# A cross-attention kernel: q of block 1 used as projected, K and V in three passes, and other places for V and for the last part of q

## The reference

```
q = x @ wq;  k = ctx @ wk;  v = ctx @ wv
scores = (q . k) / sqrt(32), masked keys set to -inf
p = softmax(scores);  a = p @ v
out = layernorm(a @ wo + x) * gamma + beta
```

## Time and profile before

| | before |
|---|---|
| median of 3 runs (lowest to highest) | 627.19 us (625.45 to 628.61) |
| profiled execution: time, span | 628.64 us, 626.8 us |
| mean granted clock of TensorE | 0.993 |
| busy in the span: TensorE, VectorE, ScalarE, GpSimd | 602.5, 514.2, 501.8, 491.5 us |
| TensorE busy by stretch: 0 to 80, 80 to 168, 168 to 180 us | 71.27, 87.90, 9.31 us |
| the same: 180 to 560, 560 to 627 us | 378.39, 55.63 us |
| DMA: moved, mean | 91.31 MB, 146 GB/s |

### The profile page before, as it was taken

One profiled execution on the slowest core, in us unless ns is written; L12 is line 12 of the kernel. 1 busy time (PEld: TensorE's weight loads), 2 busy tenths in 40 slices (PEclk: granted clock), 3 DMA queues, 4 the chain that ended last, 5 costly groups with the idle time before them and its releaser, 6 DMA issues.

```text
span 626.8 us, 12867 instructions
## 1 busy us (share of the span) xinstructions
PE 602.5 (96%) x3820; PEld 472.4 (75%) x3820; DVE 514.2 (82%) x1047; ACT 501.8 (80%) x1546; POOL 491.5 (78%) x639
## 2 busy tenths in 40 slices
PE   7998999999999999999999999999999999998995
PEld 5776587887768778787878878787877878786763
DVE  3577588988868988898889888888888888888888
ACT  4578798888868888888978988898888888787851
POOL 4477359797958979797997979798887979687784
PEclk9999999999989999999999999999999999999999
DMA  8627365464554645554464645455454545643103
GB/s 290 193 51 204 111 165 152 147 166 131 155 169 119 171 120 167 147 168 141 125 183 136 171 136 167 135 150 162 138 162 111 167 143 145 214 107 101 51 35 118
DMA packets 61717, 91.31 MB, mean 146 GB/s; under 512 B 18384, under 2 KB 19408, under 8 KB 61648
## 3 DMA queue, kind: packets, MB, share of 16 engines
q1 hardware_dynamic: 61648, 90.49, 49.5%
HBM read 39.53 MB, written 16.78 MB: 90 GB/s over the span
## 4 chain that ended last, share of the span: by engine, by line
PE 79%; DVE 6%; ACT 3%; SPq 3%; POOL 3%; DMA 3%; issue 2%; POOLq 0%; DVEq 0%; ACTq 0%
PE bank L396 26%; PE bank L492 22%; PE bank L442 7%; PE bank L432 6%; PE bank L426 5%; PE bank L465 4%; PE bank L470 2%; PE bank L446 2%; ACT pr L605 2%; DMA qd<-qn 2%; PE bank L374 2%; PE bank L388 2%; SPq L269 2%; SPq L294 1%; DVE pr L738 1%
## 5 line engine op out<-in xcount | busy, mean ns | idle before, releaser
L605 ACT ACTIVATE pr<-pr,nm 128x77 f32<-128x77 f32 x1024 | 270.0, 349 | 44.1 <-DVE nm L744 39.8
L903 POOL TENSOR_TENSOR pn<-pr,rec 128x512 f32<-128x512 f32 x128 | 134.8, 1053 | 86.7 <-DVE rec L753 81.0
L738 DVE SCALAR_TENSOR_TENSOR pr<-msk,bank 128x308 f32<-128x308 uint8 x256 | 109.8, 469 | 39.4 <-PE bank L432 34.8
L751 DVE TENSOR_REDUCE sm<-pr 128x8 f32<-128x616 f32 x128 | 100.6, 786 | 9.3 <-ACT pr L605 9.0
L744 DVE TENSOR_REDUCE nm<-pr 128x8 f32<-128x616 f32 x128 | 101.8, 795 | 4.4
L492 PE MATMUL bank<-woh,ah 128*128 128x512 f32 x256 | 104.0, 406 | 1.4 <-DVE al L760 1.4
L396 PE MATMUL bank<-xh,wqh 128*128 128x512 f32 x256 | 105.2, 411 | 0.0
L572 ACT ACTIVATE ptr<-bank 128x512 f32<-128x512 f32 (+1 forms) x256 | 95.7, 428 | 9.4 <-PE bank L442 9.3
L492 PE MATMUL bank<-wol,ah 128*128 128x512 f32 x256 | 101.4, 396 | 0.0
L492 PE MATMUL bank<-woh,al 128*128 128x512 f32 x256 | 101.3, 396 | 0.0
L396 PE MATMUL bank<-xh,wql 128*128 128x512 f32 x256 | 101.0, 395 | 0.0
(11 more groups left out here) (71 smaller groups left out, 976.6 us busy)
## 6 DMA issues: line engine op xcount, KB each, us to landing
qd<-qn SPq DMA_DIRECT2D x240, 128.0 KB, 2.6
xraw<-xT SPq DMA_DIRECT2D x58, 256.0 KB, 3.4
xres<-x SPq DMA_DIRECT2D x58, 256.0 KB, 2.9
out<-y SPq DMA_DIRECT2D x56, 256.0 KB, 2.2
ptr<-xT SPq DMA_DIRECT2D x6, 256.0 KB, 9.0
zt<-x SPq DMA_DIRECT2D x6, 256.0 KB, 4.0
out<-zt SPq DMA_DIRECT2D x6, 256.0 KB, 2.0
wk_sb<-wk SPq DMA_DIRECT2D x4, 256.0 KB, 4.5
```

The lines of the kernel that those rows point to most:

```text
L605: last = nc.scalar.activation(s, s, ACT.Exp, bias=nm[:, t % 2, h:h + 1], scale=1.0)
L738: nc.vector.scalar_tensor_tensor(out=pr[:, 4 * g:4 * g + 4, :], in0=msk[:, b % 2, t % TB, :].unsqueeze(1).broadcast_to([P, 4, LK]), scalar ...
L751: nc.vector.tensor_reduce(sm[:, t % 2, hs], pr[:, hs, :], AX.X, ALU.add).then_inc(v_sum, 1)
L903: nc.gpsimd.tensor_tensor(pn[:, half, 0:4, :].rearrange("p s (e k) -> p (s e) k", e=2), pr[:, hs, 0:KM], rec[:, t % 2, hs].unsqueeze(2).br ...
```

## The change

K and V are projected in three passes on split operands. For that wk and ctx are split at once (`keep_wk` on ScalarE, `low_wk` on VectorE), ahead of all work on wq; the high part of wk lies in the buffer of wo's high part (`woh`), those of wv and ctx in the room of `qd`, the low parts are made in place. wv is split around the first two pieces of q. The parts of V are cut one row differently (`VP`), so that each has an even number of rows.

In block 1 the scores take three full matmuls, as in block 0; q high is read from where ScalarE put it (a quarter of `qd`), and no DMA doubles it. So `double_q` begins with block 2, the low-part layout of K for batch 0 is placed at t = 4 and not at t = 1, and that of batch 1 waits until the scores of tile 7 are made. V's rows are placed in iterations 2 (batch 1), 3 (batch 2), 5 and 6 (batch 3), before in 3 to 8. At t % 16 = 15 the last piece of q is doubled between the two halves of the next batch's K, before it was behind both.

```diff
--- before.py
+++ after.py
@@ -17,6 +17,8 @@
 KR = 16
 VC = (0, P, 3 * LK, NB * LK)
+VP = ((0, P), (P, 3 * LK + 1), (3 * LK - 1, NB * LK))
 SCALE = float(np.float32(1.0) / np.sqrt(np.float32(HD)))
 EPS = 1e-5
 MASKED = -3.0e38
@@ -34,11 +36,11 @@
 VALUES = {t: STEP_OF[t - 5] for t in range(5, T - 4, 4)}
 LAG = 6
-KD_AT = {1: 0, 12: 1, TB + 4: 2, 2 * TB + 4: 3}
+KD_AT = {4: 0, 12: 1, TB + 4: 2, 2 * TB + 4: 3}
 V_AT = {1: (1,), 3: (2, range(0, 2)), 4: (2, range(2, 4))}
 V_KEPT = {2: 1, 5: 2}
-PLACE = {3: (1, 0), 4: (1, 1), 5: (2, 0), 6: (2, 1), 7: (3, 0), 8: (3, 1)}
+PLACE = {2: ((1, 0), (1, 1)), 3: ((2, 0), (2, 1)), 5: ((3, 0),), 6: ((3, 1),)}
 LAST = T - 8
 VFIN = T - 6
@@ -110,13 +112,23 @@
         ql0 = sb("ql0", [P, NG, D], f32r)
         ql1 = sb("ql1", [P, NG, D], f32r)
         with ExitStack() as start:
-            def early(name, shape):
-                return start.enter_context(nc.sbuf_tensor(name, shape, f32))
+            def early(name, shape, dt=f32):
+                return start.enter_context(nc.sbuf_tensor(name, shape, dt))
+            wvh = early("wvh", [P, KT, D], f32r)
+            ctxh = early("ctxh", [P, KT, NB * LK], f32r)
+            early("place_qd", [P, 2 * NG * D - KT * D - KT * NB * LK])
+            with ExitStack() as low:
+                wkl = low.enter_context(nc.sbuf_tensor("wkl", [P, KT, D], f32r))
+                low.enter_context(nc.sbuf_tensor("place_low", [P, 3 * KT, D], f32))
+                wvl = low.enter_context(nc.sbuf_tensor("wvl", [P, KT, D], f32r))
+                ctxl = low.enter_context(nc.sbuf_tensor("ctxl", [P, KT, NB * LK], f32r))
             wk_sb = early("wk_sb", [P, KT, D])
             wq_raw = early("wq_raw", [P, KT, D])
-            early("place_qd", [P, 2, NG, D])
             early("place_qn", [P, KT, D])
             early("place_ah", [P, KT, D])
             wv_sb = early("wv_sb", [P, KT, D])
@@ -132,7 +144,9 @@
         y = sb("y", [P, YS, D])
         ql = (ql0, ql1)
-        qk = [ah] + [qn] * (NBLK - 1)
+        wkh = woh
+        qk = [ah, qd[:, 1, 0]] + [qn] * (NBLK - 2)
         kl = kd[:, 1].rearrange("p g u k -> p g (u k)")
@@ -176,11 +190,11 @@
...
         g_z, g_vz, g_id, g_xl, g_wo, g_norm, g_c, g_ap, g_y = (
@@ -252,7 +266,7 @@
                 for i in range(3):
                     lo, hi = max(0, VC[i] - b * LK), min(LK, VC[i + 1] - b * LK)
-                    n, at = min(hi, KM) - lo, lo + b * LK - VC[i]
+                    n, at = min(hi, KM) - lo, lo + b * LK - VP[i][0]
                     if n > 0:
                         sp.dma_start(vm[KM * e + lo:KM * e + lo + n, b].rearrange("p s h d -> p s (h d)"),
                                      vs[at:at + n, i, :, e].rearrange("p s h d -> p s (h d)")).then_inc(d_vb[b], 16)
@@ -276,7 +290,7 @@
             def place_kd(b):
                 if b >= 1:
-                    sp.wait_ge(p_s, NG * max(4, TB * (b - 1)))
+                    sp.wait_ge(p_s, NG * max(8, TB * (b - 1)))
                 for v, src in enumerate((khc, klc)):
                     for j in range(4):
                         rows = slice(64 * v + 32 * (j % 2), 64 * v + 32 * (j % 2) + 32)
@@ -286,7 +300,7 @@
             def double_q(i):
                 blk, m = i // 4, i % 4
-                if blk >= 2:
+                if blk >= 3:
                     sp.wait_ge(p_s, NG * 4 * (blk - 1))
                 sp.wait_ge(a_qh, i + 1)
                 for u in range(2):
@@ -317,13 +331,14 @@
                     load_slice(t + 9)
                 if t in KD_AT:
                     place_kd(KD_AT[t])
-                if 1 <= t <= T - 4 and t % 4 > 0:
+                if 5 <= t <= T - 4 and t % 4 > 0:
                     double_q(t + 3)
                 if t % TB == TB - 1 and t < T - 1:
                     place_kh(t // TB + 1, 0)
+                if t % 4 == 3 and 7 <= t < T - 4:
+                    double_q(t + 4)
+                if t % TB == TB - 1 and t < T - 1:
                     place_kh(t // TB + 1, 1)
-                if t % 4 == 3 and t < T - 4:
-                    double_q(t + 4)
                 if t == 5:
                     sp.wait_ge(p_v, 3)
                     for o in range(XR):
@@ -333,8 +348,7 @@
                     sp.wait_ge(a_v, 1)
                     place_v(0, 0)
                     place_v(0, 1)
-                if t in PLACE:
-                    b, e = PLACE[t]
+                for b, e in PLACE.get(t, ()):
                     sp.wait_ge(a_v, (1, 2, 2, 3)[b])
                     place_v(b, e)
                 if t in (TB + 1, 2 * TB + 1):
@@ -369,24 +383,29 @@
         @block.tensor
         def _(pe):
             for k in range(KT):
-                pe.wait_ge(d_k[k], 32)
-                for g in range(NG):
-                    mm = nc.tensor.matmul(bank[g][:, 0:NB * LK], wk_sb[:, k, g * P:(g + 1) * P], ctx_sb[:, k, :],
-                                          start=(k == 0), stop=(k == KT - 1))
-                    if k == KT - 1:
-                        mm.then_inc(p_k, 1)
+                pe.wait_ge(a_wk, 2 * k + 2)
+                for n, (w, s) in enumerate(((wkh, ctxh), (wkl, ctxh), (wkh, ctxl))):
+                    if n > 0:
+                        pe.wait_ge(v_wk, 2 * k + n)
+                    for g in range(NG):
+                        mm = nc.tensor.matmul(bank[g][:, 0:NB * LK], w[:, k, g * P:(g + 1) * P], s[:, k, :],
+                                              start=(k == 0 and n == 0), stop=(k == KT - 1 and n == 2))
+                        if k == KT - 1 and n == 2:
+                            mm.then_inc(p_k, 1)
             def project_v(i, ks=range(KT)):
                 if i == 0:
-                    pe.wait_ge(d_wv, 16)
+                    pe.wait_ge(a_wv, KT)
+                    pe.wait_ge(v_wv, KT)
                 if ks[0] == 0:
                     if i < 2:
                         pe.wait_ge(v_ql, i + 3)
                     else:
                         pe.wait_ge(a_v, 1)
                 for k in ks:
-                    last = nc.tensor.matmul(AVB[i % 2][0:VC[i + 1] - VC[i], :], ctx_sb[:, k, VC[i]:VC[i + 1]], wv_sb[:, k, :],
-                                            start=(k == 0), stop=(k == KT - 1))
+                    for n, (c, w) in enumerate(((ctxh, wvh), (ctxh, wvl), (ctxl, wvh))):
+                        last = nc.tensor.matmul(AVB[i % 2][0:VP[i][1] - VP[i][0], :], c[:, k, slice(*VP[i])], w[:, k, :],
+                                                start=(k == 0 and n == 0), stop=(k == KT - 1 and n == 2))
                 if ks[-1] == KT - 1:
                     last.then_inc(p_v, 1)
@@ -416,17 +435,17 @@
                         pe.wait_ge(v_st, i - 1)
                     o = SB[i % 2]
                     cols = slice(r * P, (r + 1) * P)
-                    if blk == 0:
+                    if blk < 2:
                         if t == 0:
                             pe.wait_ge(d_kl, 64)
-                        for n, (w, s) in enumerate(((ah, kh), (ah, kl), (ql0, kh))):
+                        for n, (w, s) in enumerate(((qk[blk], kh), (qk[blk], kl), (ql[blk], kh))):
                             last = nc.tensor.matmul(o[:, 0:GW], w[:, g, cols], s[:, g, :], start=(n == 0), stop=(n == 2))
                         last.then_inc(p_s, 1)
                         continue
                     nc.tensor.matmul(o[:, 0:GW], ql[blk % 2][:, g, cols], kh[:, g, :], start=True, stop=False)
                     if r == 0:
-                        pe.wait_ge(d_qd[g], 64 * blk)
-                    if t == 4 or t > 4 and t % TB == 0:
+                        pe.wait_ge(d_qd[g], 64 * (blk - 1))
+                    if t == 8 or t > 8 and t % TB == 0:
                         pe.wait_ge(d_kd[t // TB % 2], 128 * (t // TB // 2 + 1))
                     for u in range(2):
                         last = nc.tensor.matmul(o[:, u * PW:(u + 1) * PW], qd[:, blk % 2, u, g, cols],
@@ -582,10 +601,9 @@
                 act.wait_ge(p_q, i + 1)
                 if i == 0:
                     act.wait_ge(v_w, KT)
-                if blk >= 2:
+                if blk >= 3:
                     act.wait_ge(v_ql, i - 3)
-                if blk >= 2:
-                    act.wait_ge(d_qd[m], 64 * (blk - 1))
+                    act.wait_ge(d_qd[m], 64 * (blk - 2))
                 keep(qk[blk][:, m, :], misc_bank(("q", i))[:]).then_inc(a_qh, 1)
             def keep_pt(t, half):
@@ -634,18 +652,33 @@
                                      scale=SCALE).then_inc(a_k, 1)
             def keep_v(i):
-                n = VC[i + 1] - VC[i]
+                n = VP[i][1] - VP[i][0]
                 act.wait_ge(p_v, i + 1)
                 keep(vs[0:n, i].rearrange("p s e h d -> p (s e h d)"), AVB[i % 2][0:n, :]).then_inc(a_v, 1)
+            def keep_wk(k):
+                act.wait_ge(d_k[k], 32)
+                keep(wkh[:, k, :], wk_sb[:, k, :]).then_inc(a_wk, 1)
+                keep(ctxh[:, k, :], ctx_sb[:, k, :]).then_inc(a_wk, 1)
```

(41 more changed lines are left out.)

## The result

The change is faster, by less than forecast. On the chip of the first measurement it takes 622.32 us in the median (620.88 to 623.85, 5 runs) against 625.54 for before (625.26 to 628.61, 5 runs): a ratio of 0.9935, 95% interval 0.9912 to 0.9958. On a second chip the unchanged file took 621.62 against 626.93, ratio 0.9921 (0.9899 to 0.9942). So the gain is 3.2 us on one and 5.3 on the other. The profiled execution took 622.64 us with a span of 620.8, against 628.64 and 626.8: 6.0 us less, where the sum said 7.4.

What follows compares the result with a forecast made beforehand. The prediction took TensorE's own work to bound the steady part, leaving gains at the start and where TensorE waits. From 628.64 us it took 3.9 (by tile 8), 3.4 and 0.1 (boundaries): 621.2 us, range 619.2 to 625.0.

Steps and rivals of the forecast that it cites:

- work ahead of tile 8: From the start to tile 8: the chain was to be 3.9 us early there and stay so.
- first boundary: First tile of batch 1: q piece between K's halves shortens the wait and keeps the clock up, gain 3.4 us.
- K: K's projection at the start in three passes: ends at 13.7 instead of 14.5 us, gain 0.4 us at q.
- V to tile 2: V's projection in three passes, parts 0 and 1, as far as it reaches the chain: gain 1.1 us.
- tile 4's wait: Block 1, tile 4: the wait for the fourth piece of doubled q goes, gain 1.35 us.
- clock behind it: Behind tile 4's wait: V's last part and the next projection run at the high clock level, gain 2.0 us.
- third pass: Block 1's scores: a third full matmul pass, loss 0.9 us; the skill page's formula gave 2.0 us for the block.
- second, third: First tiles of batches 2 and 3: the new order of issue gains 0.1 us at the second, nothing at the third.
- One sign of being wrong: Start of the kernel: ScalarE waiting for wv was named as showing the forecast wrong; its cover was called thin.
- Rival (a): Tile 4: the clock falls there all the same, price 1.7 us, total 622.9 us; chance 0.22.
- V's places: SyncE's queue: V placed earlier and K later, nothing in the sum, 0 to 1 us in the range.
- Rival (d): Batch boundaries: K's second half lands late behind q, waits of 2.2 to 2.9 us, total 631.4 us; chance 0.07.

Runs made afterwards that it cites:

- no_order: The changed kernel with both halves of K issued ahead of the last q piece, as before the change: 621.30 us, ratio to before 0.9928.
- v_four: The changed kernel with V projected by four-pass matmuls again: 622.14 us, ratio to before 0.9931.
- place_old: The changed kernel with V's rows placed in iterations 3 to 8, as before the change: 621.95 us, ratio to before 0.9928.
- q_first: The changed kernel with q's projection ahead of the scores of groups 2 and 3 in the first tile of batches 1, 2, 3: 628.92 us, ratio to before 1.0031.
- q_first_no_order: q_first with both halves of K issued ahead of the last q piece, as before the change: 628.77 us, ratio to before 1.0030.
- warm: The changed kernel with 11 unused matmuls of zeros on TensorE ahead of K: 623.66 us, ratio to before 0.9959.
- before_again: The kernel before, unchanged and profiled once more: 626.63 us against 626.82 for its other runs, ratio 0.9997.
- order_only: The kernel before with only the last q piece moved between the halves of K: 625.35 us against 626.82, ratio 0.9985.
- q_first group: q_first and the two kernels built on it, one with the old order of issue, one with warm's added matmuls: ratios to before 1.0031, 1.0030 and 1.0018.
- block1_only: The kernel before with only block 1 using q as projected, in three full matmuls without doubling: 624.45 us, ratio to before 0.9976.

## Why the prediction was right or wrong

The time, 621.2 us forecast and 622.32 measured, and the sign were right. The gain against the median was not 6.0 us but 3.2 on the first chip and 5.3 on the second. That the time came so near is in part luck: the work ahead of tile 8 was rightly accounted for, the 3.4 us of the first boundary had the wrong cause. Step by step, in the profile that the sum was made against:

| step | forecast | measured |
|---|---|---|
| K | 0.4 | -0.1 (the chain has q from 14.61 to 25.52, before from 14.53 to 25.43) |
| V to tile 2 | 1.1 | 1.2 (masked scores at 42.94 for 44.03, and K's 0.1) |
| tile 4's wait | 1.35 | 1.1 (V's last part at 60.05 for 62.27, less the 1.1 before) |
| clock behind it | 2.0 | 2.05 (1.39 + 2.72 for 3.25 + 2.91) |
| third pass | -0.9 | -0.8 (what is left at projection 10, 163.32 for 166.76) |
| first boundary | 3.4 | 2.5 |
| second, third | 0.1, 0 | -0.7, 0.7 |

- **K** failed in one term. I carried the low level over as the 3.2 us that before spent in it. TensorE spent 5.7 us there, 4.97 to 10.7, for a start 0.65 us later. The rise isn't a fixed time behind the start: in executions that start K between 4.84 and 5.34 us it came at 7.9 (no_order), 9.5 (v_four), 9.6 (place_old), 10.5 and 10.7 (after), 10.8 (q_first) and 11.0 (q_first_no_order). Where it came early (no_order, warm) K's 48 matmuls take 8.4 and 8.0 us instead of 9.6; but little of that reaches tile 6, since q then waits for x.
- **V, tile 4's wait, the third pass**: right within 0.3 us, and v_four confirms V in the stages (1.3 to 1.5 us up to tile 16). One sign of being wrong did come: ScalarE waited 0.8 us for wv, which landed at 17.8. It cost nothing, since its next copy of q, at 19.42, still waited 0.5 us for TensorE. The rows were right against the estimate from the page "TensorE: Matmul & The Clock Gate" of the Trainium skill, section "Back-to-back issue gap": the third pass cost 0.8 us on the path, not the 2.0 that its formula gave for the block.
- **The clock behind tile 4** was right in size and wrong as a gain that lasts. In before_again and order_only the clock stays up there, behind shorter waits on qd (0.53 and 0.31 us, against 1.02 in the first profile), and by the table of clocks only 20 of 87 runs of before have more than one fall. I had one profile, and booked as the kernel's what was that execution's. It is the likeliest reason why 2.0 us of the sum don't reach the medians. Rival (a), the clock falling at tile 4 all the same, came up in no profile of after.
- **First boundary**: the size was nearly right, the cause was wrong. I gave the 3.4 us to the order of issue. order_only doesn't have them (ratio 0.9985) and no_order doesn't lose them. The profiles point to block 1 as projected: no fall of the clock there in any kernel with it but the q_first group, and a fall in all three profiles without it. Over all runs it is a matter of how often (no fall in 10 of 12 runs of block1_only, 11 of 41 of before), and order_only's 8 of 12 can't be told from block1_only's. The remaining wait in after is SyncE's issue of K; a slow issue, not a slow landing, makes it 1.7 instead of 0.2.
- **Second boundary**: I took 0.3 us of wait and it is 0.9. The q piece between the halves waits for ScalarE's copy of it, 0.3 us, and K's half stands behind it: the queue had a gap from 306.22 to 306.62. That a wait in the middle of twelve issues holds the ones behind it was missing from the step.
- **V's places**: nothing, as forecast, but for a reason I hadn't seen. Before has a wait of ScalarE for V's last rows at tile 9 (0.7, 2.1 and 2.3 us in three profiles). The saved q DMAs end it (block1_only, place_old), not the earlier places.
- **Rival (d)**, K's half landing late behind q, didn't come: the landings were 1.8 us in after. order_only had one of 3.14, and the fall with it.

**What stays open.** Why the clock mostly stands at the first boundary in the kernels with block 1 as projected. The wait there is shorter in their profiles (0.2 to 1.7 us, against 2.2 and 2.7 in before), but block1_only stood after 1.7 and order_only fell after 1.8, and waits of 1.71 us in the q_first group ended in a fall in six cases and in none in three, so the wait's length alone doesn't decide it. Why warm has falls in half its runs (none of after's runs is on its chip), and why single DMA issues take 1.1 to 1.9 us in some executions, is open too.

## What to carry to other kernels

Profile the kernel before more than once when its runs spread over half a per cent: a fall of the clock that one execution has may be absent in the next, and a sum made against it promises too much. When a wait is to be removed by reordering, ask for each engine what stands behind the moved instruction; here 2.8 us of delay for two groups of scores became a wait on a bank and up to three falls of the clock. Where a quantity such as the granted clock is on record for every run, count with it before a profile is called typical. Taking DMAs off a queue that is always behind helped places far from the one aimed at.

## What the runs showed of the hardware

- TensorE's clock first rose at 7.6 to 8.9 us in the kernels that run K in four passes (from 3.9 to 4.3 us on), and anywhere from 7.85 to 11.0 us in kernels that started it at 4.84 to 5.34: no_order's 4.84 and after's 4.97 lie an eighth of a microsecond apart and their rises 2.9. The Trainium skill, "TensorE: Matmul & The Clock Gate", section "What's actually happening", says that the point varies by 500 ns either way with where in a free-running window the first matmul falls; the traces agree that it varies, and by more.
- Falls of the clock came after single waits of 1.7 us (six in the q_first group), 1.8 (order_only), 2.2 (before_again) and 2.7 us (before), and none after waits of 1.7 (three in the q_first group, one in block1_only and after each) and 1.9 us (warm). The fall at tile 4 in before came after two shorter waits close together, 1.2 and 1.0 us (TensorE busy 2.70 of the 5 us from 57 on); with 1.2 and 0.5 (before_again, busy 3.18 of 5) or 0.3 (order_only, 3.41) there was none. Each fall lasted 3.4 us in the granted clock and cost about 1.6 (the projection behind it took 4.24 and 4.39 us instead of 2.79).
- Issues of the same small DMA by SyncE took 0.6 us as a rule and up to 1.9 us now and then.
